# Index columns for gathers: copied one step ahead, or copied and waited for in the same step

## The reference

```python
# L0: attention with 4 heads per edge, then a feed-forward block and two column norms
feat = leaky(xl[src] + xr[dst]); logits = einsum('ehc,hc->eh', feat, att)
alpha = segment_softmax(logits, dst); out = segment_sum(alpha * xl[src], dst)
...
# L1: edges weighted by their type, in both directions
out = segment_sum(w * support[col], row) + segment_sum(w * support[row], col) + bias
# L2: two convolutions of this kind
agg = segment_sum(x[src] @ W_msg + b_msg, dst); h = agg + x @ W_self + b_self
# L3: attention with 8 heads
e = leaky(s_u[src] + s_v[dst]); out = segment_sum(xh[src] * softmax(e, dst), dst)
```

## Time and profile before

| | |
|---|---|
| median of 3 runs | 10775.97 us (10763.34 to 10826.26) |
| the profiled execution, its own time | 10739.69 us |
| its span, first to last instruction | 10737.9 us |
| mean granted clock of TensorE | 0.723 |
| GpSimd busy | 5352.2 us, 50% of the span |
| TensorE busy with matmuls | 6092.5 us, 57% |
| VectorE busy | 4834.7 us, 45% |
| DMA queue of GpSimd's gathers and scatters | 26.7% of 16 engines |

### The profile page before, as it was taken

One profiled execution on the slowest core, in us unless ns is written; L12 is line 12 of the kernel. 1 busy time (PEld: TensorE's weight loads), 2 busy tenths in 40 slices (PEclk: granted clock), 3 DMA queues, 4 the chain that ended last, 5 costly groups with the idle time before them and its releaser, 6 DMA issues. The chain is left out here.

```text
span 10737.9 us, 135754 instructions
## 1 busy us (share of the span) xinstructions
PE 6092.5 (57%) x24674; PEld 4803.9 (45%) x24675; DVE 4834.7 (45%) x13534; ACT 2017.8 (19%) x5480; POOL 5352.2 (50%) x5364
## 2 busy tenths in 40 slices
PE   4788886775656666645554555555555642222376
PEld 2777774554444444433332343334343432222254
DVE  6344446776544444445554333343233411112777
ACT  2111111783322222200000000010000300000276
POOL 3555551000078888866664666636666146664000
PEclk9688877997877777766666676677676755555699
DMA  4555555662077777754443333222323156665265
GB/s 148 160 165 162 161 162 190 199 201 80 18 111 105 105 105 104 105 125 135 133 135 100 88 88 87 87 78 86 86 86 87 40 154 195 194 197 158 72 201 181
DMA packets 835352, 1362.46 MB, mean 127 GB/s; under 512 B 112278, under 2 KB 488660, under 8 KB 834980
## 3 DMA queue, kind: packets, MB, share of 16 engines
q0 software_dynamic: 315328, 634.04, 26.7%
q1 hardware_dynamic: 385684, 562.46, 16.0%
q10 hardware_dynamic: 133968, 161.50, 4.7%
HBM read 943.05 MB, written 414.50 MB: 126 GB/s over the span
## 5 line engine op out<-in xcount | busy, mean ns | idle before, releaser
L1014 POOL DMA_INDIRECT rows_in<-table,gather_rows x2352 | 2250.9, 957 | 1276.4 <-issue 618.2
L1111 PE MATMUL ps_p<-rows_in,hot 128*128 x5280 | 1783.1, 494 | 1708.2 <-issue 758.9
L1111 PEld LDWEIGHTS ps_p<-rows_in,hot 128*128 128x128 f32 x5280 | 1236.8, 247 | 2211.0 <-issue 2014.6
L1740 POOL DMA_INDIRECT scatter_sums<-regionC,idx x880 | 1384.3, 1573 | 306.5 <-issue 248.1
L959 DVE TENSOR_TENSOR regionC<-regionC,ps_p 128x257 f32 (+2 forms) x1320 | 558.2, 423 | 1537.7 <-DVEq L956 846.1
L1014 POOL DMA_INDIRECT regionB<-table,gather_rows x784 | 783.4, 999 | 637.6 <-POOLq L1011 431.5
L1480 PE MATMUL ps_p<-regionA 128*128 128x265 f32 (+1 forms) x3520 | 849.0, 394 | 335.6 <-PEq L1475 215.0
L1014 POOL DMA_INDIRECT regionC<-table,gather_rows x784 | 759.7, 969 | 476.8 <-POOLq L1011 242.9
L1945 PE MATMUL psS<-dst_scores,regionA 128*128 x1760 | 393.3, 362 | 882.7 <-PEq L1943 648.8
L1480 PEld LDWEIGHTS ps_p<-regionA 128*128 128x128 f32 x3520 | 654.0, 191 | 530.6 <-DVE regionC L959 194.0
L1945 PEld LDWEIGHTS psS<-dst_scores,regionA 128*128 128x128 f32 x1760 | 383.6, 330 | 892.4 <-issue 892.4
(11 more groups left out here) (304 smaller groups left out, 7652.8 us busy)
## 6 DMA issues: line engine op xcount, KB each, us to landing
regionA<-edge_rows SPq DMA_DIRECT2D x880, 256.0 KB, 3.2
edge_rows<-regionB SPq DMA_DIRECT2D x196, 512.0 KB
edge_rows<-regionC SPq DMA_DIRECT2D x392, 256.0 KB
regionC<-srcrow_d SPq DMA_DIRECT2D x220, 256.0 KB
scatter_sums<-zero_rows ACTq DMA_DIRECT2D x8, 6400.0 KB, 41.5
regionA<-scatter_sums ACTq DMA_DIRECT2D x49, 1024.0 KB
rows_in<-table,gather_rows POOLq DMA_INDIRECT x2352
regionB<-rrow_d ACTq DMA_DIRECT2D x110, 256.0 KB
```

Source lines behind the costliest of these rows:

```text
L1014: g.indirect_dma_start(out=rows_of(b * per + j), out_offset=None, in_=table, in_offset=bass.IndirectOffsetOnAxis(ap=idx[:, column:column + ...
L1111: x = te.matmul(ps[(u.c * VG + j) % NB][:, 0:width], hot[:, b, 2 * j + k, :], at_tile(G, slot[j] * 2 + k), start=k == 0, stop=k == 1)
L1740: g.indirect_dma_start(out=scat, out_offset=bass.IndirectOffsetOnAxis(ap=idx[:, b, j:j + 1], axis=0), in_=sums[:, b, j, :], in_offset=None ...
```

## The change

The loop in `gather` no longer runs one step ahead. Before, a turn waited for the copy of the turn before, made the copy for the next gathers, and issued the gathers of the copy that had been waited for. Now a turn makes its copy, waits for it and issues the gathers from it.

```diff
-            for t_ in turns(g, steps, ring, 1):
-                if t_.has(1):
-                    g.wait_ge(own_p, 1)
-                    g.sem_inc(own_p, -1)
-                if t_.has(0):
-                    bring(t_.at(0))
-                if t_.has(1):
-                    fetch(t_.at(1))
+            for t_ in turns(g, steps, ring, 0):
+                bring(t_.at(0))
+                g.wait_ge(own_p, 1)
+                g.sem_inc(own_p, -1)
+                fetch(t_.at(0))
```

## The result

The changed kernel is a little faster: 10714.11 us against 10817.52 us for the kernel before, run beside it (medians of 7 runs each), a ratio of 0.9921 with an interval of 0.9895 to 0.9946. The forecast of 10929 us and its range miss it, on the wrong side.

What follows compares the result with a forecast made beforehand. No engine fills a gather pass; it cycles through gather runs, a full ring and stops. 186 - 11 - 22 = +153 us on the median of 10776 gave 10929 us, range 10765 to 11000.

Steps and rivals of the forecast that it cites:

- The price: GpSimd, between copy and gather: 0.92 us where 0.16 stood, so +0.76 us a step where the gather follows closely.
- close gathers: Gathers that begin within 0.3 us of their copy: 303 of 436, with 58 of them in att0.
- The cheap wait: Rival, chance 0.12: the gather starts 0.17 us after the copy, so the change costs 3 us, 10779 us in all.
- The step that failed: Plain passes: a longer run of gathers delays the full ring, the burst of adds and the freed places equally.
- 33 us (11 and 22): Plain passes, deductions: 11 us for 1.8% fewer stops, 22 us for 20 stops under 2 us that swallow the shift.
- The stops: GpSimd's waits for a ring place in plain passes: expected to stay near 150, of about 4 us each.
- the crawl: Consumers of the ring working slowly while gathers are issued without a break: two adds 7.03 us apart.
- The hidden case: Rival, chance 0.22: ring places come free at fixed moments, so the waits absorb the added time; 10776 to 10800 us.
- The faster case: Rival, chance 0.11: pauses free the consumers; 10627 us at three more adds per pause, 10345 with the ring never full.
- att0 at nothing: Pass att0: cost put at nothing, since ring waits follow in most steps; 44 us if that cover were gone.
- where I deducted nothing: Pass att3: nothing taken off the price, as its runs and stops repeat in the same cycle; 24 us longer.
- The round that the loop makes more in each pass: Loop without its written-out first round, once more per pass: costed at nothing, 4 us if in the open.

Runs made afterwards that it cites:

- e5: The changed kernel itself, measured again on another chip: ratio 0.9886 to the kernel before.
- e8: The kernel before with TensorE's streams of the plain passes as hardware loops instead of written out: ratio 1.0004 to the kernel before.
- e3: The kernel before, order kept, plus a small copy that is waited for in front of each step: ratio 0.9846 to the kernel before.
- e11: The kernel before plus four small copies that nothing waits for in front of every 4 gathers: ratio 0.9879 to the kernel before.
- e13: The kernel before plus six small copies that nothing waits for in front of every 4 gathers: ratio 0.9594 to the kernel before.
- e7: The changed kernel with a waited copy in front of each group, every 4 gathers (8 in att3): ratio 0.9644 to the kernel before.
- e9: The changed kernel with a waited copy in front of every 4 gathers in all five passes: 10380.59 us, ratio 0.9603 to the kernel before.
- e2: The kernel before with the new order in att0 and att3 alone: ratio 0.9935 to the kernel before.
- e1: The kernel before with the new order in the three plain passes alone: ratio 0.994 to the kernel before.
- e12: The kernel before with gathers of 512 bytes instead of 1,024 per row number in the plain passes: ratio 1.0004 to the kernel before.
- e14: The kernel before with SyncE's loop over the groups as a hardware loop instead of written out: ratio 1.0016 to the kernel before.
- e6: The changed kernel with its copy made and waited for four times in each step: ratio 0.9834 to the kernel before.
- e10: The changed kernel with a waited copy in front of every 2 gathers in all five passes: ratio 1.0155 to the kernel before.

## Why the prediction was wrong

**The price was right.** 0.92 us between copy and gather were forecast, 0.88 measured; 303 x 0.76 = 230 us would have been the price of all close gathers, and e5 against e8 measures 249, since with fewer stops more pauses lie in the open (322 gathers of e5 begin within 1.1 us of their copy, 252 of them in the plain passes, where I counted on 303 and 214). The cheap wait is thereby refuted. The rule that I set beside it, in the Trainium skill, Perfetto Trace Analysis, section DMA Instruction — SWDGE (GPSIMD), has the instruction decoded before it waits, from which I took that the gather would follow at once; in these traces it follows 0.88 us behind the copy.

**The step that failed** is "in such a cycle a longer run shifts the stop, the burst and the release with it". From it I gave back only 33 us (11 and 22) of the price. The ring's waits gave back 343 us, ten times as much. The stops did not stay "about as many and as long as now": 141 became 123, 620 us became 444.

**Why the step failed.** I took the crawl as a fixed pace and judged a pause by whether a burst follows it at once. The rows on that were read rightly: a single pause late in a run brings no burst before the change, and the adds of after show the same. But pauses work on the pass as a whole: with more time in breaks there is less of the crawl, and with enough of it next to none. e3, e11 and e13 show this, since they add breaks alone to the kernel before, and e7 and e9 with the changed order. I had written down the chance that it turned on, that "the crawl of the consumers changes its pace because gathers come 7% less densely", and gave it neither a chance nor a price, because no row of before could show it. A lack of rows was no evidence against it.

**The hidden case** looked right by its own sign on the two profiles of before and after: ring waits of the plain passes "from 613 us towards 450", passes as long as before. It is not what happened: a place that comes free at a fixed moment can't make e3 faster, and on one chip (e8, e5) each plain pass is 18 us shorter. The two profiles mislead: the profiled execution of before, 10739.69 us, is shorter than all seven runs of before beside the changed kernel (10763.34 to 10826.26), so their spans, 7 us apart, say less than the ratio.

**The faster case**, with 0.11, had the direction and the size: its break-even was 1.3 adds more per pause, at 0.47 us of stops for an add. In e5 the plain passes gave back 233 us over 252 pauses in the open, 0.92 us each, which is 2.0 adds by that count. But its own sign did not show: the adds don't gather in the pauses (0.24 per us in the pauses of under 1.6 us of the changed kernel, 0.36 over the plain passes), and the stops got fewer by an eighth (141 to 123), not by a third. That consumers run better over the whole pass is what the runs show; that they catch up in each pause, as this case had it, they don't.

**att0 at nothing** was wrong as well, to the better. e5 has it 30 us shorter than e8 and the changed kernel 10 us shorter than before, about as much as unchanged kernels differ (1438 to 1472); e2, against e1 on one chip, has it 96 us shorter and e9 169, which is clear of that. It comes without the sign seen in the plain passes: att0 has 11 register instructions of over 0.3 us in e8 and 9 in e9. What the windows of att0 show, of e8 and of e9:

```profile
262.00:1713.00 1451.00, 1224.14 (x6762) 1106.14 (x6762) 655.63 (x1060) 250.04 (x422) 805.25 (x880) 0.78 0.51 161
```

```profile
263.00:1545.00 1282.00, 1140.62 (x6775) 1025.23 (x6776) 655.82 (x1059) 249.87 (x422) 833.43 (x979) 0.84 0.59 182
```

TensorE is busy for 84% of the pass and then for 89%, its mean granted clock goes from 0.78 to 0.84 (between its levels of 1.2 GHz, 0.5, and 2.4 GHz, 1.0), and as many matmuls take 1141 us instead of 1224, by the ratio of the clocks (0.93). So half of the 169 us is a higher clock's and half is idle time of TensorE that has gone. Which of the two brought the other, these runs don't tell.

**att3**, where I deducted nothing, paid 36 us for its pauses and got 46 back: it is 11 us shorter in e5 than in e8, where 24 us more were forecast (the changed kernel has it 6 us longer than before, so no more than the missing price is clear). The round that the loop makes more in each pass is not seen as a cost of its own in these sums.

**What stays open** is what the gathers meet the consumers in: the register instructions of SyncE and TensorE, and the hand-over from TensorE to VectorE. Shown is that the slowness goes with the density of gathers in time, not with their bytes (e12), nor with the written-out streams (e8, e14), nor with what stands dispatched on GpSimd (e13). In att0 and att3, where the gain came without drawn-out register instructions, the link between the breaks and the consumers is not traced.

## What to carry to other kernels

When consumers crawl while one engine issues without a break, that engine's pace can be part of the cause: a pause must be costed for what the others do better with it, and a few idle copies in front of each batch are a cheap test of it (e13: 4% faster with 5,880 copies that nothing uses). Judge such a pause by the whole pass, not by what follows one pause in the trace. And where traces of two kernels come from different chips, take the sum from a pair on one chip.

## What the runs showed of the hardware that was not expected

- Some 900 of the 7,604 register instructions of SyncE and TensorE in the plain passes of the kernel before last 0.6 to 0.8 us, a few up to 1.4 us, where the median is 0.055 us; GpSimd issues indirect gathers 1.25 us apart there (0.95 and 0.30). On VectorE the longest of these takes 0.12 us; ScalarE has none in these passes.
- In the same passes VectorE's add begins up to 5 us and more after the last matmul ahead of it has ended in the profile, with VectorE idle: 993 us in all before, 28 in e6, none over 1 us in e10.
- How many are drawn out falls steeply between e11 and e13: 515 with 0.83 us without a gather every 4 gathers, 33 with 1.07 us. That is a gather every 1.39 us (4 x 0.96 + 3 x 0.30 + 0.83, over 4) and every 1.45 us; the two ran on different chips. With about the time of e13 in one piece every 8 gathers (e6, 2.16 us) there are 75.
- Half the bytes per gather change nothing: 954 ns a gather on GpSimd and a ratio of 1.0004 in e12.
